# First stage of a four-layer sLSTM decoder in a new order on all engines: layers six steps apart, cell in the gate banks, interleaved head statistics, biases on 64-row tiles

## The reference

```python
def _ln(x, w):                      # over the 256 features
    ...
for l in range(4):
    x = x + slstm(_ln(x, ln1_w[l]), ...)      # 4 heads of 64
    x = x + ffn(_ln(x, ln2_w[l]), ...)        # gelu(x @ up[:, :336]) * (x @ up[:, 336:]) @ down
return _ln(x, post_w)

# slstm: xc = silu(causal depthwise conv of 4 taps + bias)
# gates i, f from xc; z, o from the normed x (64x64 per head)
def step(carry, wx_t):
    h, c, n, m = carry
    raw = wx_t + einsum('bhd,hdgo->bhgo', h, rk) + b
    ir, fr, zr, og = raw[:, :, 0], raw[:, :, 1], raw[:, :, 2], raw[:, :, 3]
    lfm = m + log_sigmoid(fr)
    mn = maximum(ir, lfm)
    ig = exp(ir - mn); fg = exp(lfm - mn)
    cn = fg * c + ig * tanh(zr)
    nn = fg * n + ig
    hn = sigmoid(og) * cn / nn
    return (hn, cn, nn, mn), hn
# then each head of h is normed over its 64 features and scaled by gn_w
```

## Time and profile before

| | us |
|---|---|
| three runs | 4048.97, 4050.81, 4053.24 (median 4050.81) |
| span of the profiled execution, first to last instruction | 4046.7 |
| of it: up to the first step of the first stage | about 48 |
| the 284 steps | about 2463 |
| from there to the end (second stage) | about 1533 |

### The profile page before, as it was taken

One profiled execution on the slowest core, in us unless ns is written; L12 is line 12 of the kernel. 1 busy time (PEld: TensorE's weight loads), 2 busy tenths in 40 slices (PEclk: granted clock), 3 DMA queues, 4 the chain that ended last, 5 costly groups with the idle time before them and its releaser, 6 DMA issues. The chain is left out here.

```text
span 4046.7 us, 170045 instructions
## 1 busy us (share of the span) xinstructions
PE 3876.7 (96%) x70778; PEld 2189.0 (54%) x70778; DVE 3681.0 (91%) x10771; ACT 3256.1 (80%) x6720; POOL 2211.6 (55%) x2425
## 2 busy tenths in 40 slices
PE   6999999999999999999999998799999999999997
PEld 3555555555555555555555554466666666666664
DVE  7999999999999999999999998788888888888886
ACT  4999999999999999999999998466666666666665
POOL 3666666666666666666666666444344443444443
PEclk9999999999999999999999999899999999999998
DMA  2000111000000000000000000000000001000000
GB/s 77 21 23 23 48 54 51 21 23 23 21 23 23 21 23 23 21 23 23 21 23 23 21 23 24 17 22 23 31 24 23 23 22 33 23 22 22 26 21 9
DMA packets 101034, 105.27 MB, mean 26 GB/s; under 512 B 17536, under 2 KB 96032, under 8 KB 99768
## 3 DMA queue, kind: packets, MB, share of 16 engines
q1 hardware_dynamic: 100264, 94.39, 8.0%
HBM read 48.68 MB, written 17.69 MB: 16 GB/s over the span
## 5 line engine op out<-in xcount | busy, mean ns | idle before, releaser
L596 POOL TENSOR_TENSOR conv_products<-normed_features,conv_taps_by_token 128x256 f32<-128x256 f32 (+1 forms) x852 | 780.4, 916 | 609.7 <-DVE convolved_features L549 358.5
L309 PE MATMUL banks<-up_centred,after_cell_features 128*32 128x336 f32 x9088 | 759.6, 452 | 0.0
L786 POOL TENSOR_TENSOR exps_of_both_halves<-scores 128x256 f32<-128x256 f32 x512 | 419.1, 842 | 619.9 <-ACT scores L1042 614.7
L285 PE MATMUL banks<-down,hidden_features 112*32 112x256 f32 x6816 | 427.5, 384 | 0.0
L365 ACT ACT_TABLE_LOAD x284 | 364.4, 1283 | 52.7 <-PE banks L265 47.8
L586 POOL TENSOR_TENSOR conv_partial_sums<-conv_products,conv_partial_sums 128x512 f32<-128x512 f32 x284 | 364.8, 1285 | 66.6 <-DVEq L485 44.4
L1042 ACT ACTIVATE scores<-scores 128x512 f32<-128x512 f32 x512 | 305.4, 626 | 116.3 <-DVE scores L1190 115.4
L309 PEld LDWEIGHTS banks<-up_centred,after_cell_features 128*32 128x32 f32 x9088 | 237.2, 109 | 270.6 <-issue 270.6
L386 ACT ACT_TABLE_LOAD x284 | 364.4, 1283 | 5.0
L1190 DVE SCALAR_TENSOR_TENSOR scores<-banks,score_top 128x512 f32<-128x512 f32 x512 | 327.7, 681 | 27.0 <-PE banks L872 26.4
L258 PE MATMUL banks<-recurrent_weights,h_features 64*32 64x256 f32 x9088 | 311.7, 383 | 1.4 <-ACT h_features L358 1.4
(11 more groups left out here) (215 smaller groups left out, 10055.6 us busy)
## 6 DMA issues: line engine op xcount, KB each, us to landing
layer_inputs<-layer_outputs SPq DMA_DIRECT2D x284, 96.0 KB, 2.0
layer_inputs<-in_x SPq DMA_DIRECT2D x285, 32.0 KB, 1.8
x_scratch<-layer_outputs SPq DMA_DIRECT2D x284, 32.0 KB, 1.8
x_tokens<-in_x SPq DMA_DIRECT2D x32, 256.0 KB, 3.1
context_features<-in_ctx SPq DMA_DIRECT2D x32, 256.0 KB, 3.8
layers_out<-x_scratch SPq DMA_DIRECT2D x32, 256.0 KB, 2.9
...
```

The source lines that it names most:

```text
L285: mm = nc.tensor.matmul(bank[group(l), FD, 0:D], hidt[:, i, group(l)], down[:, l, i, :], start=i == 0, stop=i == UTILES - 1, skip_group_ch ...
L309: mm = nc.tensor.matmul(bank[group(l), b, 0:UP], xmt[:, n, group(l)], up[:, l, n, at:at + UP], start=n == 0, stop=n == HALF - 1, skip_grou ...
L596: nc.gpsimd.tensor_tensor(prod[:, i:i + n], xnt[:, j % NRING].rearrange("p n t -> p (n t)")[:, None, :].broadcast_to([P, n, HALF * P]), ta ...
L786: nc.gpsimd.tensor_tensor(psum[:, i % RING, :], pr[:, i % RING, 0:S], pr[:, i % RING, S:2 * S], ALU.add).then_inc(halves_added, 1)
```

## The change

- The layers are six steps apart in place of seven, with `LEAD` 2: `STEPS` becomes 256 + 23 = 279.
- The loops of PE, DVE, ACT and POOL have a new order, and each step's instructions are cut at other places (DVE now begins a step with `dl`, PE with the transposes of `xm` and `xn`). PE does feed-forward up in two whole halves (gate half, value half).
- `add_bias` makes eight fp16 matmuls of 64 rows x 32 columns (two for each layer) in place of two of 12 rows x 128 columns. The rows that hold no bias are zero.
- The cell stands in the z gate's place in the gate banks; tanh of z and of o are written in place there, and so is the growth logarithm (in the f gate's place of the step before).
- The copy of the transposed h moves from ACT to DVE (a multiply by 8), and h is kept scaled by 1/8.
- The head statistics are two `bn_stats` over two heads interleaved element by element, whose even and odd results are the two heads' own; the four `bn_aggr` go.
- After step `STARTED` = 21 two scalars that were read from a tile (`begun`, `never`) are a constant and nothing.
- POOL's loop has no waits on DVE; it waits on its own instructions and on the copy of `xn`.
- SP waits one step less for `xm_done`; the moved rows go one ring place ahead.
- Before the loop there are more memsets, and the bias rows are copied to partition 64.

The removed lines of the loops are those printed above; of the diff the new ones stand here.

```diff
-LAG = 7
-LEAD = 4
-STEPS = 284
-FIRST = LEAD + 3 * LAG + 3
+LAG = 6
+LN1_BEHIND, OUT_BEHIND = 4, 3
+LEAD = LAG - LN1_BEHIND
+FIRST = LEAD + 3 * LAG + OUT_BEHIND
+STEPS = S + FIRST
+STARTED = LEAD + 3 * LAG + 1
 XROWS = STEPS + 2
-XRING, NRING, MRING, ORING = 7, 4, 4, 4
+XRING, NRING, MRING, ORING = 6, 4, 4, 4
...
-            sy.dma_start(bias[32:32 + 3 * LAYERS, :], bias[0:3 * LAYERS, :]).then_inc(bias_moved, DMA)
-            sy.dma_start(pick16[32:32 + 3 * LAYERS, :], pick16[0:3 * LAYERS, :]).then_inc(bias_moved, DMA)
+            sy.dma_start(bias[64:64 + 3 * LAYERS, 512:BIAS], bias[0:3 * LAYERS, 512:BIAS]).then_inc(bias_moved, DMA)
+            sy.dma_start(pick16[64:64 + 3 * LAYERS, :], pick16[0:3 * LAYERS, :]).then_inc(bias_moved, DMA)
...
-                sy.dma_start(xr[group(0), (j + 4) % XRING, :], row(a["x"], j + 1)).then_inc(x_loaded, DMA)
+                reach(sy, xm_done, j - 1)
+                reach(sy, x_loaded, DMA * j)
+                sy.dma_start(xr[group(0), (j + 1) % XRING, :], row(a["x"], j + 1)).then_inc(x_loaded, DMA)
                 sy.wait_ge(xo_done, j + 1)
-                if j > 0:
-                    sy.wait_ge(x_moved, DMA * j)
-                    sy.wait_ge(x_stored, DMA * j)
-                sy.dma_start(xr[32:128, (j + 3) % XRING, :], xo[0:96, j % ORING, :]).then_inc(x_moved, DMA)
+                reach(sy, x_moved, DMA * j)
+                reach(sy, x_stored, DMA * j)
+                sy.dma_start(xr[32:128, (j + 1) % XRING, :], xo[0:96, j % ORING, :]).then_inc(x_moved, DMA)
...
-            def add_bias(b, r, at, n):
-                rows_ = slice(32 * r, 32 * r + 3 * LAYERS)
-                return nc.tensor.matmul(bank[:, b, 0:n], pick16[rows_, :], bias[rows_, at:at + n], start=True, stop=False,
-                                        skip_group_check=True)
...
+            def add_bias(j):
+                for l in range(LAYERS):
+                    for odd in range(2):
+                        r = slice(DH * odd, DH * odd + DH)
+                        mm = nc.tensor.matmul(bank[group(l), 2 * (j % 2) + odd, :], pick16[r, group(l)], bias[r, 512 * odd:512 * odd + 512],
+                                              start=True, stop=False, skip_group_check=True)
+                return mm
...
+            add_bias(1).then_inc(first_gates, 1)
             for j in range(STEPS):
...
+                reach(pe, xm_done, j)
+                transposes(CV, D, xm[:, (j - 1) % MRING], xmt_ready)
+                transposes(CV, 0, xn, xnt_ready)
+                add_bias(j)
+                by_head(j, wg, xnt[:, (j - 1) % NRING], 2, GATES)
+                pe.wait_ge(xmt_copied, j + 1)
+                feed_up(UPG, 0).then_inc(g_done, 1)
+                pe.wait_ge(h_done, HALF * (j + 1))
                 transposes(FD, D, h, ht_ready)
...
                 pe.wait_ge(xnt_copied, j + 1)
...
+                hidden_features().then_inc(hidt_ready, 1)
+                pe.wait_ge(xs_done, j + 1)
+                by_head(j, wg, xst, 0, 2)
+                pe.wait_ge(ht_copied, j + 1)
+                by_head(j, rk, ht, 0, GATES).then_inc(rec_done, 1)
+                centred().then_inc(cen_ready, 1)
+                pe.wait_ge(hidt_copied, j + 1)
+                feed_down().then_inc(down_done, 1)
+                pe.wait_ge(yn_done, j + 1)
+                feed_up(UPV, UP).then_inc(up_done, 1)
...
                 act.wait_ge(d_ready, j + 1)
                 nc.scalar.activation(td[:], dl[:], ACT.Tanh, scale=-0.5).then_inc(td_done, 1)
...
+                reach(act, yn_done, j)
+                reach(act, rstd_done, j)
+                nc.scalar.activation(gl[:], bank[:, UPG, 0:UP], ACT.Gelu, scale=rs2).then_inc(gelu_done, 1)
+                act.wait_ge(xnt_ready, j + 1)
+                copy(both(xmt[:]), bank[:, CV, D:]).then_inc(xmt_copied, 1)
+                copy(both(xnt[:, j % NRING]), bank[:, CV, 0:D]).then_inc(xnt_copied, 1)
                 act.wait_ge(conv_done, j + 1)
                 nc.scalar.activation(ct[:], part[:, j % 2, 0], ACT.Tanh).then_inc(ct_done, 1)
+                nc.scalar.preload_act_table_set(LOG_EXP)
+                nc.scalar.activation(spb[:], dl[:], ACT.Exp).then_inc(growth_exp, 1)
+                act.wait_ge(growth_exp, j + 1)
+                act.wait_ge(h_done, HALF * (j + 1))
+                nc.scalar.activation(gate(j - 1, 1), heads(spb[:]), ACT.Ln, bias=1.0).then_inc(growth_log, 1)
                 act.wait_ge(hidt_ready, j + 1)
...
+                copy(both(hidt[:]), bank[0:UT, CV, 0:UTILES * P]).then_inc(hidt_copied, 1)
+                act.wait_ge(ln1_mv, j + 1)
+                nc.scalar.activation(lrs[:], variances, ACT.Ln, bias=eps[:]).then_inc(log_rstd_done, 1)
+                act.wait_ge(log_rstd_done, j + 1)
+                nc.scalar.activation(rstd[:], lrs[:], ACT.Exp, scale=-0.5).then_inc(rstd_done, 1)
+                act.wait_ge(rec_done, j + 1)
+                nc.scalar.activation(heads(fb[:]), gate(j, 1), ACT.Exp).then_inc(f_exp, 1)
+                act.wait_ge(f_exp, j + 1)
+                nc.scalar.activation(fb[:], fb[:], ACT.Ln, bias=1.0).then_inc(f_log, 1)
+                nc.scalar.preload_act_table(ACT.Gelu)
+                act.wait_ge(sf_done, j + 1)
+                nc.scalar.activation(gate(j, 3), gate(j, 3), ACT.Tanh, scale=0.5).then_inc(o_done, 1)
+                nc.scalar.activation(gate(j, 2), gate(j, 2), ACT.Tanh).then_inc(z_done, 1)
...
+            dve.wait_ge(first_x, DMA)
+
+            def ratio_to_h(j, n):
+                return nc.vector.scalar_tensor_tensor(out=h[:, n * P:(n + 1) * P].rearrange("p (r d) -> p r d", r=2),
+                                                      in0=gates_of(j - 1)[:, :, n, 3, :], scalar=1.0, in1=heads_of(half_r[:], n),
...
+                cell = gate(j - 1, 2)
+                reach(dve, sf_done, j)
+                nc.vector.scalar_tensor_tensor(out=dl[:], in0=v[:], scalar=-60.0, in1=sf[:], op0=ALU.max,
+                                               op1=ALU.subtract).then_inc(d_ready, 1)
+                reach(dve, xm_done, j)
+                nc.vector.bn_stats(stat2[:], xm[:, (j - 1) % MRING]).then_inc(ln2_stat, 1)
+                reach(dve, z_done, j)
+                nc.vector.scalar_tensor_tensor(out=cell, in0=heads(half_r[:]), scalar=-2.0 / H_SCALE, in1=cell, op0=ALU.mult,
+                                               op1=ALU.add).then_inc(cell_added, 1)
+                dve.wait_ge(cell_added, j + 1)
+                dve.wait_ge(td_done, j + 1)
+                nc.vector.scalar_tensor_tensor(out=cell, in0=heads(td[:]), scalar=1.0, in1=cell, op0=ALU.add,
+                                               op1=ALU.mult).then_inc(cell_scaled, 1)
+                dve.wait_ge(ln2_stat, j + 1)
+                nc.vector.bn_aggr(mv2, stat2[:]).then_inc(ln2_mv, 1)
+                dve.wait_ge(cell_scaled, j + 1)
+                nc.vector.scalar_tensor_tensor(out=heads(half_r[:]), in0=cell,
+                                               scalar=0.25 * H_SCALE if j >= STARTED else begun[:, j:j + 1],
+                                               in1=heads(half_r[:]), op0=ALU.mult, op1=ALU.add).then_inc(ratio_done, 1)
+                dve.wait_ge(ratio_done, j + 1)
+                ratio_to_h(j, 0).then_inc(h_done, 1)
+                dve.wait_ge(gelu_done, j + 1)
+                reach(dve, up_done, j)
+                nc.vector.scalar_tensor_tensor(out=hid[:], in0=bank[:, UPV, 0:UP], scalar=rs2, in1=gl[:], op0=ALU.mult,
+                                               op1=ALU.mult).then_inc(hid_done, 1)
+                ratio_to_h(j, 1).then_inc(h_done, 1)
+                dve.wait_ge(ct_done, j + 1)
+                nc.vector.scalar_tensor_tensor(out=xst[:].rearrange("p n t -> p (n t)"), in0=ct[:], scalar=1.0, in1=part[:, j % 2, 0],
+                                               op0=ALU.add, op1=ALU.mult).then_inc(xs_done, 1)
+                reach(dve, x_moved, DMA * j)
+                reach(dve, x_loaded, DMA * j)
+                nc.vector.bn_stats(stat1[:], xr[:, j % XRING, :]).then_inc(ln1_stat, 1)
+                dve.wait_ge(ht_ready, j + 1)
+                nc.vector.tensor_scalar(ht[:].rearrange("p n t -> p (n t)"), bank[:, FD, D:], 1.0 / H_SCALE, None,
+                                        ALU.mult).then_inc(ht_copied, 1)
+                for n in range(HALF):
+                    dve.wait_ge(h_done, HALF * j + n + 1)
+                    nc.vector.bn_stats(head_stat[:, n, :], h[:, n * P:(n + 1) * P].rearrange("p (r d) -> p d r", r=2)).then_inc(gn_stat, 1)
+                dve.wait_ge(ln1_stat, j + 1)
+                nc.vector.bn_aggr(mv1, stat1[:]).then_inc(ln1_mv, 1)
+                dve.wait_ge(growth_log, j + 1)
+                nc.vector.scalar_tensor_tensor(out=heads(sp[:]), in0=gate(j - 1, 1), scalar=40.0, in1=heads(dl[:]), op0=ALU.min,
                                                op1=ALU.max).then_inc(grown, 1)
```

(32 more changed lines are left out.)

259 lines of the change are left out of this document (59 added, 200 removed).

## The result

The changed kernel takes 3760.55 us (median of four runs, 3758.06 to 3761.6); beside it the kernel before took 4052.02 (4048.97 to 4053.61, four runs). The ratio is 0.9279, 95% interval 0.9266 to 0.9293: faster by 291.5 us, where 3826 meant a gain of about 226. It lies inside the range of 3745 to 3920.

A forecast was written before the change was run, and what follows sets the result against it. Full PE and DVE queues were taken to bound the old kernel; first `dl` 48, 278 x 8.03 = 2232, last step 9 and second stage 1533 gave span 3822, median 3826 us, range 3745 to 3920 (own range 3790 to 3870).

The forecast's parts named there:

- What bounds before: Old step of 8.674 us: PE's and DVE's queues are both full, so a gain needs shorter queues on both.
- PE's unit prices and its new queue: PE per step: prices per wave and per tile shape change, six changes instead of eleven, sum 7.72, 0.95 less.
- DVE's half ring: DVE from the start of `dl` through the cell to the end of h's second half at 3.37 us.
- the walk: Four engine queues carried forward until the step repeats: 8.03 us new, closed by DVE, PE's middle, DVE; old order 8.70.
- The holds: DVE instructions with two SBUF inputs end 0.29 after an overlapping POOL instruction; `xm` and `dl` together 0.57 a step.
- Line 532's hold: DVE line 532, held 0.36 by a POOL product, is freed by putting cell and tanh in the gate banks.
- No holds: Rival, 0.13: POOL drifts into DVE's gaps, PE's queue of 7.72 decides the step, 3740 us.
- Longer holds: Rival, 0.17: a held DVE instruction takes its whole 0.42 after POOL's end; 8.42 a step, 3935 us.
- The bias tiles run in a row: Slower rival, 0.05: PE's eight bias tiles run one behind another, 1.7 us, PE queue 9.18, 4146 us.
- The sum: First `dl` 48, 278 steps of 8.03 are 2232, last step 9, second stage 1533: span 3822, median 3826 us.
- New waits: `growth_log`'s wait for h costs nothing; moved rows have cover 1.6 us; ACT's busy time becomes 7.5.
- The marks I had set: Profile signs: DVE line 8.0 apart, bias under 0.3, PE idle before transposes of h and `xm`, `dl` near 0.78, `xm` 0.62.

The follow-up runs named there:

- up_half: Changed kernel without half the contraction of up's value half (8 of 16 matmul records) on PE; 3731.6 us, a step of 7.693.
- dve_filler: Changed kernel with one more `bn_stats` of `xm` on DVE behind the real one, result unused; 3889.88 us, a step of 8.259.
- tanh_sbuf: Changed kernel with tanh of z and o written to SBUF again, as in the kernel before; 4203.95 us, a step of 9.392.
- hidden_after_gates: Changed kernel with the transposes of the hidden features moved behind the second gates on PE; 3970.82 us, a step of 8.551.
- bias_12_rows: Changed kernel with the bias put back to two full-width matmul tiles of 12 rows; 3796.67 us, a step of 7.933.
- lag7: Changed kernel with layers seven steps apart again, 282 steps, rings of seven rows; 3782.13 us, a step of 7.780.
- centred_between: Changed kernel with each half's centring issued between the halves of the recurrence on PE; 3782.8 us, 0.9343 of the kernel before.

## Why the prediction was right or wrong

**What bounds before: wrong in its reason, without harm.** "PE's queue is full" rested on distances from start to start, which in the earlier trace rows hold a wait of 0.14 ahead of the transposes of `xm` (the gates' 0.81 is 0.66 or 0.67 of work and that wait). That gates with the same columns cost 0.64 two rows further down was the sign. The new sum took the gates at 0.55, from the unit prices, so the mistake didn't reach it. That a gain had to come from shorter queues on both engines held, and more: ACT's ring had to go too, and the new order, with the copy of `xm` behind the first gates, did that unbooked.

**PE's unit prices and its new queue: right.** 7.72 forecast, 7.75 measured. By the rows: four transposes 0.59 (0.55), bias 0.22 (0.24), gates 0.57 (0.55), up 1.27 (1.25), five transposes 0.70 (0.69), gates 0.46, recurrence 0.86 (0.89), centring 0.52, down 1.32, up 1.24 (1.25). The price of a change of shape, worked out as what is left of 24 and of 8 records, carried six of them to 0.03.

**DVE's half ring: right in size.** From the cell addition (1510.35) to the end of h (1512.67) are 2.32; the walk had 2.35 (1.02 to 3.37). The copy of h and the head statistics cost nothing extra (0.33 to 0.34 and 0.40 for two, 0.20 each where I took 0.18). But it isn't the path: h is ready 0.23 before PE asks for it, and PE waits for it only in other kernels (`up_half`, `dve_filler`, `tanh_sbuf`).

**The holds: the step that failed.** "Together 0.21 + 0.36 = 0.57 a step on the chain" measured 0.08 on `dl` and nothing on `xm`. Their kind was right: `xst` and `dl` end 0.28 and 0.29 after POOL's end, as the 0.29 of the earlier trace rows said. What failed is POOL's phase. I let the double product start 2.27 after `dl` and the last addition end at 8.52; it starts at 2.08 (1511.68 - 1509.60) and the addition ends at 7.95 (1509.80, with the `dl` before at 1509.60 - 7.75 = 1501.85). The start is 0.19 early, and the rest is in the joints: independent POOL instructions start up to 0.04 before the one ahead has ended, where I put a gap between all of them. So `xm` came at the end of the double addition and not in its middle. Line 532's hold did go, but not for the reason given: `tanh_sbuf` runs its successor at 0.41 with two SBUF inputs, since POOL is idle there in the new order. That was luck. Without those 0.5 us of hold DVE's chain is shorter than 7.75, and PE's queue decides.

**Rivals.** *No holds* named the right limit and gave 3740; the 20 us up to 3760.55 are 0.03 of work and 0.03 of occasional holds a step (16 us), and the rest behind the last step. Its reason ("three instructions can hardly all miss it") was half met: `xst` is held each step, off the path. *Longer holds* fell: no held instruction took its whole 0.41 after POOL's end. The Trainium skill, "SBUF — State Buffer", section "Who interferes with whom", says that order of issue decides who blocks. The rows agree: `xm` ahead by 0.05 makes POOL's addition 0.95, behind by 0.02 it takes 0.99 itself. The page also counts `tensor_scalar` among the operations that can use the shared pair; `xn` in `hidden_after_gates` is held (1285 ns against 407), and I had passed it over. Whether it runs in the mode that the page ties this to is not shown: its plain 407 ns is no less than the 401 of the copy of h from PSUM. What the page states of the whole instruction did not show as a whole duration after the release in any row here. *The bias tiles run in a row* fell: eight take 0.22.

**The sum.** The first `dl` was at 47.1 (48). 278 steps at 7.779 are 2163 (2232). From the last `dl` to the end 1549.8 (1542): the first matmul of the second stage comes 1.3 later after its POOL wait (9.85 idle against 8.51 before), and the second stage, same code, took some 6 us more (1531.5 from its first matmul to the end, against 1525.4). That stage varied by itself, from the first to the last start of its first projection's line 1459.6 us in `bias_12_rows`, 1464.0 in `lag7`, 1465.8 here, 1460.4 before; why wasn't followed up. The runs stood 1.05 above the profiled span instead of 4.1. In all 65.5: 69.8 for the steps and 0.9 for the start, less 7.8 behind them, and 3 for the profiled execution against the median, with 0.4 of rounding.

**New waits: right.** `growth_log` waits for nothing, and the moved rows held nobody up. But ACT's busy time (7.5 forecast, 1699.96 / 1800 x 7.779 = 7.35 measured) hid how near ACT is: it waits 0.26 for the recurrence each step, its tanh of z is done 0.08 ahead of the cell addition, and a recurrence that ended 0.14 later made the step 7.85 (`centred_between`).

**The marks I had set.** 279 instructions a line, bias under 0.3, line 532's successor near 0.43, POOL's addition across the start of `dl`: seen, and `yn` waiting for PE too (it starts at 1507.80, 0.04 after the centring ends and 0.47 after `xn`, where 0.33 would do). A DVE line 8.0 apart, PE idle ahead of the transposes of h and of `xm`, `xm` near 0.62: not seen; PE is idle nowhere, and `xm` at its plain time was the one of the three that I had listed as a sign of being wrong.

**Open.** Which of the rings near 7.64 binds once PE has room, and why `xm` is held most often every 32nd step, is not shown. Whether freedom from holds and less work on PE together would go below 7.64 wasn't tried, nor was line 532's successor alone in the old order, or the wait of the `xm` transposes moved alone there. No kernel here beats the changed one with its full computation.
